# Four stages of an audio-tower kernel: rows loaded five or six pairs ahead, and a pair's steps spread over six and five slots

## The reference, cut to what matters

```python
# layer 1 attention: retention
ret = einsum('bqd,bkd->bqk', rope(X @ W_Q), rope(X @ W_K)) * D;  h += ret @ (X @ W_V)
# layer 2 attention ("third attention"): q, k, v are thirds of the token axis, 83 tokens each
e = einsum('bmc,hc->bmh', x, W) + b;  q, k, v = split(e, 3, axis=1)     # 3 heads
o = softmax(q k^T * SCALE) v;  out = concat(heads) @ W_out.T + b_out;  h += out + x
# layer 2 feed-forward ("depths"): the top half of the tokens by a score goes through an MLP
w = x @ wr + br;  idx = top_k(w, k)[:kk]
y = gelu_tanh(x[idx] @ w1 + b1) @ w2 + b2;  processed[idx] = y * w[idx];  h += processed + x
```

## Time and profile before

| | |
|---|---|
| runs | 4483.22, 4476.45, 4478.4 us (median 4478.4) |
| profiled execution | 4477.33 us, of which the span from first to last instruction is 4475.6 us |
| granted TensorE clock | 0.907 on average |
| busy: PE, PEld, DVE, ACT, POOL | 86%, 59%, 63%, 52%, 46% |
| retention, first to last H1 | 873.1 to 1035.3 us |
| attention 2, first to last H1 | 2162.0 to 2433.2 us |
| depths 2, first to last H1 | 2459.2 to 2682.1 us |

### The profile page before, as it was taken

The page is one execution under the profiler, slowest core; times in us unless marked ns, Lnnn a source line. Parts: engine busy times, 40 slices in busy tenths (PEclk is TensorE's granted clock), DMA queues, the critical chain, the costliest instruction groups (busy, mean ns, idle before and its releaser), DMA issues.

```text
span 4475.6 us, 111341 instructions
## 1 busy us (share of the span) xinstructions
PE 3860.8 (86%) x31697; PEld 2637.7 (59%) x31697; DVE 2821.6 (63%) x9288; ACT 2319.8 (52%) x5869; POOL 2070.4 (46%) x2404
## 2 busy tenths in 40 slices
PE   7488847697999799999666778999999999899999
PEld 7355533485666566666665445666666666555555
DVE  2577735675788544444344767888888888455554
ACT  5455524322444344443232335888888888555555
POOL 0143437664655422221676654555555555444443
PEclk9999966697999899999555678999999999899999
DMA  2111123331111333333111220000000000333332
GB/s 52 37 30 30 28 46 98 82 71 41 38 36 36 69 75 86 76 76 72 35 42 45 53 55 14 12 11 12 14 13 12 11 12 9 68 77 75 76 76 58
DMA packets 483330, 207.55 MB, mean 46 GB/s; under 512 B 452850, under 2 KB 473326, under 8 KB 482930
## 3 DMA queue, kind: packets, MB, share of 16 engines
q1 hardware_dynamic: 483058, 204.73, 20.3%
HBM read 158.75 MB, written 45.91 MB: 46 GB/s over the span
## 4 chain that ended last, share of the span: by engine, by line
PE 53%; issue 16%; POOL 11%; DVE 9%; SPq 6%; DMA 2%; ACT 2%; POOLq 0%; DVEq 0%; ACTq 0%
POOL att_P L3565 5%; PE sw_pH L4167 5%; PE moe_pH L2725 5%; PE sw_pY L4154 4%; PE moe_pY L2748 4%; PE att_pP L3674 3%; PE att_pS L3662 3%; PE att_pS L980 3%; PE att_pO L3691 3%; DVE att_M L1175 3%; PE moe_pH L2729 2%; PE moe_pH L2735 2%; PE att_pS L2218 1%; SPq L2892 1%; PE att_pO L1042 1%
## 5 line engine op out<-in xcount | busy, mean ns | idle before, releaser
L3565 POOL TENSOR_TENSOR att_P<-att_P,att_rden 125x498 f32<-125x498 f32 x512 | 521.0, 1018 | 510.0 <-DVE att_rden L3860 509.3
L3753 ACT ACTIVATE att_P<-att_Z,att_nb 125x249 f32<-125x249 f32 x1024 | 501.7, 494 | 32.3 <-issue 27.3
L2790 DVE TENSOR_TENSOR moe_hT<-moe_silu,moe_pH 128x498 f32<-128x498 f32 x384 | 258.8, 674 | 312.6 <-ACT moe_silu L2774 312.6
L4215 ACT ACTIVATE sw_hT<-sw_pH,sw_b 128x498 f32<-128x498 f32 x512 | 318.4, 673 | 220.0 <-PE sw_pH L4167 220.0
L3674 PEld LDWEIGHTS att_pP<-att_ident,att_P 124*125 124x125 f32 (+1 forms) x2048 | 262.5, 187 | 234.5 <-issue 234.5
L3674 PE MATMUL att_pP<-att_ident,att_P 124*125 124x124 f32 (+1 forms) x2048 | 349.5, 293 | 50.7 <-issue 37.6
L3872 DVE CUSTOM_DVE_ANT_0 att_Z<-att_pS,att_mask 125x249 f32<-125x249 f32 x1024 | 365.9, 412 | 29.6 <-PE att_pS L3662 27.3
L2774 ACT ACTIVATE moe_silu<-moe_pH 128x498 f32<-128x498 f32 x384 | 225.3, 587 | 262.6 <-PE moe_pH L2729 176.9
L3760 ACT ACTIVATE att_PTr<-att_pP 125x498 f32<-125x498 f32 x512 | 296.7, 579 | 76.0 <-PE att_pP L3674 69.3
L2701 POOL TENSOR_TENSOR moe_xe<-moe_share,moe_x 128x1992 f32<-128x1992 f32 x32 | 130.0, 4064 | 430.3 <-DMA moe_share<-mixing 403.4
L4074 POOL TENSOR_TENSOR sw_acc<-sw_acc,sw_Z 128x249 f32<-128x249 f32 x224 | 154.6, 690 | 363.9 <-DVE sw_Z L4294 363.2
(11 more groups left out here) (463 smaller groups left out, 9755.1 us busy)
## 6 DMA issues: line engine op xcount, KB each, us to landing
moe_share<-mixing SPq DMA_DIRECT2D x64, 498.0 KB, 6.2
sw_share<-mixing SPq DMA_DIRECT2D x64, 498.0 KB, 5.7
ffn_W<-in_ffn_pairs SPq DMA_DIRECT2D x64, 192.0 KB, 2.4
att_F<-h_stream SPq DMA_DIRECT2D x192, 62.5 KB
att_X<-h_stream SPq DMA_DIRECT2D x192, 62.5 KB
h_stream<-att_H SPq DMA_DIRECT2D x64, 62.5 KB
ffn_F<-h_stream SPq DMA_DIRECT2D x64, 62.5 KB
ret_F<-h_stream SPq DMA_DIRECT2D x64, 62.5 KB
```

The lines of the kernel that those rows point to most:

```text
L2790: v.tensor_tensor(hT[:, u, k, :, :], sl[:, k % 3, :, :], pH[:, k % 3, :, T:2 * T], ALU.mult).then_inc(*hid_ready.one())
L3565: g.tensor_tensor(own, own, bc(rden[:, j % 2, c, :], T), ALU.mult).then_inc(*scaled.one())
L3753: ins = a.activation(P[:, r, c, t, :], Z[:, r, c, t, :], ACT.Exp, scale=-1.0, bias=nb[:, r, c, t:t + 1], accum_out=den[:, r, c, t:t + 1])
L4215: a.activation(hT[:, k % 4, :, :], pH[:, place, :, 0:T], ACT.Relu, bias=b1[:, k:k + 1]).then_inc(*hid_ready.one())
```

## The change: what it does

- `opened` only loads pairs 0 and 1. The loads of pairs 2 up to the lead move from the opening into `streamed` (in attention 1, attention 2 and switch 3 into the stage's own stream), so on SP they now come after the closing stores of the stage before and after the wait for their landing. This concerns six borders: into retention, attention 1, attention 2, depths, attention 3 and switch 3.
- Retention and depths: lead 5 instead of 4. Third attention: lead 6 instead of 4, and `keep` ahead of `ahead` in the loop.
- Third attention: six parts of five steps instead of four parts of four. The square goes from GpSimd to ScalarE, the final sum H1 from GpSimd to VectorE.
- Depths: five parts of five steps instead of three parts of four. The square goes from GpSimd to ScalarE; base, scale and final sum get steps in another order.

```diff
-def opened(sp, ahead, keep, lead=4):
+def opened(sp, ahead, keep):
     for n in range(2):
         ahead(sp, n, n)
         keep(sp, n, n)
+def streamed(sp, ahead, keep, store, lead=4):
     for n in range(2, lead):
         ahead(sp, n, n % 2)
-def streamed(sp, ahead, keep, store, lead=4):
     whole = (PAIRS - lead) // 2
     with sp.Fori(0, whole) as j:
         for u in range(2):
             n = j * 2 + u
-            ahead(sp, n + lead, u)
+            ahead(sp, n + lead, (u + lead) % 2)
             store(sp, n, u)
             keep(sp, n + 2, u)
     for n in range(2 * whole, PAIRS - 2):
+        if n + lead < PAIRS:
+            ahead(sp, n + lead, (n + lead) % 2)
         store(sp, n, n % 2)
         keep(sp, n + 2, n % 2)
...
@@ retention 1
-            sp.wait_ge(*before["stored"].after(2, 0))
-            sp.wait_ge(*before["stored"].after(3, 1))
-            opened(sp, ahead, keep, 4)
+            sp.wait_ge(*before["stored"].after(0, 0))
+            sp.wait_ge(*before["stored"].after(1, 1))
+            opened(sp, ahead, keep)
...
-            streamed(sp, ahead, keep, store, 4)
+            streamed(sp, ahead, keep, store, 5)
...
@@ attention 2, SP's stream
-            with sp.Fori(0, (PAIRS - 4) // 2) as j:
+            for n in range(2, 6):
+                ahead(sp, n, n % 2)
+            with sp.Fori(0, (PAIRS - 6) // 2) as j:
                 for u in range(2):
                     n = j * 2 + u
-                    ahead(sp, n + 4, u)
                     keep(sp, n + 2, u)
+                    ahead(sp, n + 6, u)
                     store(sp, n, u)
-            for n in (PAIRS - 4, PAIRS - 3):
+            for n in range(PAIRS - 6, PAIRS - 2):
                 keep(sp, n + 2, n % 2)
                 store(sp, n, n % 2)
...
@@ attention 2, who does what in which part (GpSimd, TensorE, ScalarE, VectorE)
-            waves(g, (pre, nothing, soft, ends), STEPS)
+            waves(g, (nothing, even, turn_in, nothing, soft, nothing), STEPS)
-            waves(pe, (nothing, proj, soft, ends), STEPS)
+            waves(pe, (nothing, nothing, turn_in, proj, soft, ends), STEPS)
-            waves(a, (nothing, proj, soft, nothing), STEPS)
+            waves(a, (nothing, even, turn_in, proj, soft, nothing), STEPS)
-            waves(v, (pre, proj, soft, ends), STEPS)
+            waves(v, (pre, nothing, turn_in, proj, soft, ends), STEPS)
...
@@ depths 2, GpSimd
-            def pre(n, u, step):
-                if step == 0:
+            def even(n, u, step):
+                if step == 2:
                     g.wait_ge(*xn_ready.before(n))
                     norm.center(g, n, g4(Fi[:, u, :, :, :]))
-                    norm.square(g, n)
-                if step == 2:
+            def turn_in(n, u, step):
+                if step == 1:
                     norm.power(g, n)
-                if step == 3:
...
                     norm.scale(g, n, g4(xn[:, u, :, :, :])).then_inc(*xn_ready.one())
             def main(n, u, step):
-                if step == 1:
+                if step == 0:
...             # base
-                if step == 3:
+                if step == 4:
...             # final sum H1
-            waves(g, (pre, lambda n, u, step: None, main), STEPS)
+            waves(g, (nothing, even, turn_in, nothing, main), STEPS)
@@ depths 2, TensorE: transposes at step 3 of turn_in, scores and hidden at step 2 of proj, pT at step 4 of main
-            waves(pe, (lambda n, u, step: None, proj, main), STEPS)
+            waves(pe, (nothing, nothing, turn_in, proj, main), STEPS)
@@ depths 2, ScalarE
+            def even(n, u, step):
+                if step == 4:
+                    norm.square_scalar(a, n)
-            waves(a, (lambda n, u, step: None, proj, main), STEPS)
+            waves(a, (nothing, even, turn_in, proj, main), STEPS)
@@ depths 2, VectorE: sums at step 4 of pre, variance at step 0 of turn_in, counts at step 1, res at step 3 of main
-            waves(v, (pre, lambda n, u, step: None, main), STEPS)
+            waves(v, (pre, nothing, turn_in, nothing, main), STEPS)
```

More of the change, by code:

```diff
@@ L2055, in _ @@
             const(sp, cl, ties[:, :], every_row(A["const_ties"], PT))
-            sp.wait_ge(*before["stored"].after(4, 0))
-            sp.wait_ge(*before["stored"].after(5, 1))
+            sp.wait_ge(*before["stored"].after(0, 0))
+            sp.wait_ge(*before["stored"].after(1, 1))
             for n in range(2):
@@ L3113, in pre, with turn_in @@
             def pre(n, u, step):
+                if step == 4:
+                    v.wait_ge(*loaded.after(n, u))
+                    v.wait_ge(*norm.centered.before(n))
+                    norm.sums(v, n, g4(F[:, u, :, :, :]))
+            def turn_in(n, u, step):
                 if step == 0:
-                    v.wait_ge(*loaded.after(n, u))
-                    norm.sums(v, n, g4(F[:, u, :, :, :]))
-                if step == 2:
                     norm.spread(v, n, 1e-5)
             def proj(n, u, step):
-                if step == 1:
+                if step == 2:
                     v.wait_ge(*a_done.after(n))
@@ L3148, in ends @@
                                     bc(rden[:, :], C), ALU.mult).then_inc(*o_ready.one())
-            waves(v, (pre, proj, soft, ends), STEPS)
+                    v.wait_ge(*o_ready.after(n))
+                    v.wait_ge(*base_ready.after(n))
+                    v.wait_ge(*stored.lagging(n, u))
+                    st.held(v)
+                    v.tensor_tensor(g4(H1[:, u, :, :, :]), tmp[:, :, :], g4(base[:, u, :, :, :]),
+                                    ALU.add).then_inc(*h_ready.one())
+            waves(v, (pre, nothing, turn_in, proj, soft, ends), STEPS)
         yield
@@ L3188, in stage_depths2, with nothing @@
         base = st.sb("base", [PT, 4, C])
+        def nothing(n, u, step):
+            pass
         const_loaded = st.event("const_loaded", dma=True)
@@ L4009, in _ @@
             const(sp, cl, first[:, :], every_row(A["const_first"], PT))
-            sp.wait_ge(*before["stored"].after(2, 0))
-            sp.wait_ge(*before["stored"].after(3, 1))
-            for n in range(4):
+            sp.wait_ge(*before["stored"].after(0, 0))
+            sp.wait_ge(*before["stored"].after(1, 1))
+            for n in range(2):
                 ahead(sp, n, n % 2)
@@ L4022, in _ @@
         def _(sp):
+            for n in range(2, 4):
+                ahead(sp, n, n % 2)
             for n in range(2):
```

86 lines of the change are left out of this document (41 added, 45 removed).

## The result

The kernel after takes 4398.5 us (median of four runs, 4397.2 to 4401.7) against 4477.4 before (median of four runs): ratio 0.982, 95% interval 0.9804 to 0.9835, or 79 us. 4418 was forecast, 4396 to 4462 as the range. The profiled execution after took 4401.7 us, the longest of the four, with a span of 4399.9, 75.7 less than before.

A forecast was written before the change was run, and what follows sets the result against it. It took SP's DMA issue to bound attention 2, a ring of waits depths, and F's landings to delay retention. 4477.3 - 8.8 (retention) - 5 (border into depths) - 47.7 (depths) + 1.5 (attention 3) = 4417.3, plus 1.1: 4418; range 4396 to 4462.

The forecast's parts named there:

- Depths: Depths' steady state: the new order cuts the ring of waits; 7.19 to 5.65 us per pair, 47.7 us gained.
- Its 5.34 us is the floor of the period: Depths: VectorE's 15 instructions without a gap, 5.34 us, set the shortest possible period per pair.
- What is late next is VectorE's train: Depths: once the ring is cut, VectorE's same 15 instructions, 5.34 us, bind next.
- TensorE's slow spells: Depths: spells of TensorE at clock 0.50, allowed for by 0.3 us per pair above the 5.34 floor.
- Attention 2: Third attention: SP's 18 DMAs per pair keep the period at 9.135 us; only beginning and end give 8.7 us.
- The start of depths: Border into depths: later loads turn the 8.7 us gained before it into 5 us at depths' first H1.
- Retention: Retention: lead 5 takes F's landing off the chain, 5.23 to 4.80 us per pair; 13.3 gained, 4.5 lost at start.
- A: Rival, depths: TensorE at 1.2 GHz becomes the bound at 7.0 us per pair, 4460 us; chance 0.15.
- B: Rival, depths: Square beside Gelu_apprx_tanh makes ScalarE change tables twice per pair, 31 us lost, 4497 us; chance 0.03.
- C: Rival, depths: the new order makes its own ring over ScalarE's square, period 7.9, 4488 us; chance 0.06.
- D: Rival, attention 2: SP is not the true limit; deeper slots bring some 7.2 us per pair, 4368 us; chance 0.04.
- E: Rival: steady states stay because of another, missed ring; only the ends shift, 4470 to 4480 us; chance 0.06.

The follow-up runs named there:

- E7: Kernel after, but in depths GpSimd's scale waits until VectorE has ended the four counts of the pair beside it: 4407.5 us, ratio 0.9846.
- E8: Kernel after, but in depths TensorE makes pT of the older pair ahead of pX: 4391.5 us, ratio 0.9814.
- E10: Kernel after with early loads (retention, depths), four DMAs per transfer (attention 2), pT before pX and X's load before the store (depths): 4316.7 us.
- E5: Kernel after, with four DMAs per transfer in attention 2 instead of six, same bytes and rows: 4334.9 us, ratio 0.9679.
- E4: Kernel after, with loads of pairs 2 and 3 back ahead of the closing stores in retention and depths: 4386.3 us, ratio 0.9792.
- E6: Kernel before, with four DMAs per transfer in attention 2 instead of six: 4465.5 us, ratio 0.9973.
- E3: Kernel after, with depths' square back on GpSimd behind the centering: 4396.3 us, ratio 0.9816.

## Why the prediction was right, and where not

**The sum.** The time came 2.5 us inside the lower end of the range and below the forecast's own 4400 to 4445: 79 us were gained where 60 were forecast. The forecast is 11.5 us short in depths and 5.9 in retention; the other terms differ by some 2 us or less each.

**Depths, right in kind, low in size.** 47.7 us were forecast and 59.2 came. The step that failed is "Its 5.34 us is the floor of the period": the stage runs at 163.7/31 = 5.28, below it. The 15 durations were read where GpSimd's work lay beside each count; the change moved that work, and three counts of four fell from about 0.85 to 0.48; the whole train became 4.86. The step "What is late next is VectorE's train" fell as well. A ring through pX and pT was next (E7 and E8), then the landing of X (E8 and E10). Only in E10, at 4.99, does the chain run mainly through VectorE; that nothing else binds there was not tested by a run. The forecast's floor was too high by 0.48 us per pair, and the ring held the stage 0.42 above the real one. That these two errors nearly cancelled, so that 5.28 came out close to 5.34, is luck. Most of what the term lacked, some 9 of the 11.5 us, is the 0.3 us per pair added for TensorE's slow spells. The clock rose from 0.71 to 0.87 and TensorE's busy time fell from 5.56 to 128.54/31 = 4.15 us per pair; no run isolates the spells that are left.

**Attention 2, right.** The period stayed: from the store of pair 1 (2154.15) to that of pair 25 (2374.22) SP's timeline has 24 periods of 9.17 us, against 9.135. E5 shows that it was SP. Beginning and end together gave 8.2 us where 8.7 were forecast; but their split was wrong, the beginning was 2.8 earlier and not 1.5 later, and the stage itself gave 5.4.

**The start of depths, right.** 3.7 us of loss were forecast and 4.7 measured; E4 shows the cause, the loads of pairs 2 and 3 behind the closing stores.

**Retention, low.** Net 8.8 forecast, 14.7 measured. The start cost 4.1 (forecast 4.5). The mis-sized term is the period: 4.80 from TensorE's 4.76 us of busy time per pair before; it came to 143.4/31 = 4.63, with TensorE busy 141.75 of 143 us. VectorE's waits for F, 29.1 us before, are gone, as forecast. TensorE's busy time per pair fell by 0.2 at the same clock of 0.99; a busy time read while the engine also waits was no exact floor.

**The other borders.** Into attention 1 +1.1 and into switch 3 +0.3 us, inside the plus or minus 2; into experts 1, for which nothing was forecast, -2.2. Into attention 3 it was 3.4 lost instead of 1.5; the same border has 98.9 to 102.2 in the kernels with the same code there.

**The rivals.** A did not come: 0.87, not 1.2 GHz. B did not: the Gelu line of depths still has one table load in all, so Square and Gelu_apprx_tanh are served by one table. C came in another shape: the new order did make its own ring, over pT behind pX instead of ScalarE's square, but a shorter one than the old. D is refuted: the period stayed at 9.17, and with fewer DMAs and nothing else changed it fell to 204.6/31 = 6.6 (E5). E did not come: the periods of retention and depths both fell.

## What to carry to other kernels

A train of instructions read from a trace is a floor only for the neighbours it had: ask which durations would change when another engine's work moves. When a ring is cut, look for the next one in the new program order on each engine before taking an engine's busy time as the bound. And deepening the slots of a stage gains nothing per pair while a queue paces it: count the DMAs per pair first. Here one regrouping of them was worth 64 us in the new form of attention 2 (E5) and 11 in the old (E6), so each of the two changes needed the other.

## What the runs showed of the hardware

- VectorE's counts (two inputs in SBUF) take 0.47 to 0.48 us alone and 0.8 to 0.9 when a GpSimd instruction of 256 columns lies beside most of their length; the gate of 4 columns takes 0.16 alone and 0.47 beside one, the short step L637 0.17 alone and, in the mean, 0.38 (before) or 0.62 (after) beside one. The row sums (0.41) and `res`, which reads PSUM (0.42), keep their times beside one (in E3 26 of 32 `res` lie beside one). The Trainium skill (SBUF — State Buffer, Who interferes with whom) has a VectorE instruction with two SBUF inputs and a GpSimd instruction that reads SBUF contend for one port pair, and leaves a reduction alone; by that rule the counts stretch and the row sums do not, and the traces agree (0.48 against 0.85 in E7 and after). GpSimd's power reads SBUF too, so by the rule it should stretch the counts as well. It does not: the 60 counts beside it in the kernel after take 0.47 to 0.48, and the measurement decides.
- SP's price of a DMA in attention 2's loop is 0.42 to 0.45 us whether its rows come in two pieces or in three (six in 2.67, four in 1.69 to 1.81; half of them move 80 rows and half 3).
- In E5 TensorE was busy 98.63 of 100 us in attention 2 and was still granted 0.50, which is 1.2 GHz; in retention of the kernel after it was busy 141.75 of 143 us at 0.99. So a busy TensorE alone did not bring the higher clock there.
